# The opening of a gated cross-attention and MoE kernel: ctx laid out transposed, Wk in four quarters on SyncE's queue, x's first pair normed alone

## The reference

```python
q = (layernorm(x) @ Wq);  k = (context @ Wk * SCALE);  v = (context @ Wv)
attn = softmax(q k^T)                                   # 16 heads, 64 context tokens
x = x + tanh(g_xattn[0]) * ((attn v) @ Wo + bo)
h = layernorm(x);  probs = softmax(mean_t(h) @ gate_w);  top 2 experts, weights normed
x = x + tanh(g_ffn[0]) * sum_e combine[e] * (gelu(h @ w1[e] + b1[e]) @ w2[e] + b2[e])
```

## Time and profile before

| | |
|---|---|
| median of 3 runs | 322.09 us |
| the profiled execution, its time | 321.86 us |
| its span | 319.8 us |
| TensorE busy | 314.9 us, 98% |
| VectorE busy | 233.9 us, 73% |
| ScalarE busy | 164.1 us, 51% |
| GpSimd busy | 78.7 us, 25% |
| TensorE's granted clock | 1.0 of full speed throughout |

### The profile page before, as it was taken

One profiled execution on the slowest core, in us unless ns is written; L12 is line 12 of the kernel. 1 busy time (PEld: TensorE's weight loads), 2 busy tenths in 40 slices (PEclk: granted clock), 3 DMA queues, 4 the chain that ended last, 5 costly groups with the idle time before them and its releaser, 6 DMA issues.

```text
span 319.8 us, 5745 instructions
## 1 busy us (share of the span) xinstructions
PE 314.9 (98%) x1881; PEld 272.6 (85%) x1881; DVE 233.9 (73%) x563; ACT 164.1 (51%) x577; POOL 78.7 (25%) x158
## 2 busy tenths in 40 slices
PE   8999999999999999999999999999999999999996
PEld 8978988989999999888788888888887899888896
DVE  1989997988889999999998475466767554442643
ACT  2658556686765768766366254444543442321320
POOL 1416548484465535425600000000000000000000
PEclk9999999999999999999999999999999999999999
DMA  7991000000000027500016250000020000000011
GB/s 275 382 162 6 1 2 0 2 1 3 0 0 3 0 83 251 196 1 0 2 8 255 78 186 1 0 0 0 22 101 11 2 0 2 0 0 0 2 65 66
DMA packets 20765, 17.35 MB, mean 54 GB/s; under 512 B 11068, under 2 KB 16900, under 8 KB 20612
## 3 DMA queue, kind: packets, MB, share of 16 engines
q1 hardware_dynamic: 20464, 16.51, 17.2%
q10 hardware_dynamic: 276, 0.52, 0.5%
HBM read 14.93 MB, written 2.10 MB: 53 GB/s over the span
## 4 chain that ended last, share of the span: by engine, by line
PE 88%; DVE 7%; DMA 2%; issue 1%; ACT 1%; SPq 0%; DVEq 0%
PE ps L1105 26%; PE ps L1106 26%; PE ps L1107 26%; PE ps L1190 4%; DMA xt<-in_x_dram 2%; PE ps L1279 1%; PE ps L1125 1%; DVE mx L857 1%; PE ps L1163 1%; DVE pT_lo L815 1%; PE ps L1221 1%; PE ps L1377 1%; ACT sx L587 1%; DVE stats L736 1%; DVE sm L826 1%
## 5 line engine op out<-in xcount | busy, mean ns | idle before, releaser
L674 ACT ACTIVATE gel<-ps,b1sel 128x512 f32<-128x512 f32 x64 | 43.9, 690 | 95.5 <-PE ps L1107 95.4
L1064 DVE CAST h_hi<-gel 128x512 fp32r<-128x512 f32 x64 | 28.4, 444 | 58.7 <-ACT gel L674 58.4
L587 ACT ACTIVATE sx<-ps,mx 128x64 f32<-128x64 f32 x128 | 38.3, 327 | 27.6 <-DVE mx L857 27.6
L1105 PE MATMUL ps<-yT_hi,w_hi 128*128 128x512 f32 (+1 forms) x128 | 50.5, 395 | 0.0
L1106 PE MATMUL ps<-yT_lo,w_hi 128*128 128x512 f32 (+1 forms) x128 | 50.0, 391 | 0.0
L1107 PE MATMUL ps<-yT_hi,w_lo 128*128 128x512 f32 (+1 forms) x128 | 49.9, 390 | 0.0
L1066 DVE TENSOR_TENSOR h_lo<-gel,h_hi 128x512 fp32r<-128x512 f32 x64 | 44.9, 702 | 2.2
L473 POOL TENSOR_TENSOR sx<-sx,rs 128x512 f32<-128x512 f32 x32 | 33.1, 1056 | 48.1 <-DVE rs L831 48.0
L1105 PE MATMUL ps<-h_hi,w_hi 128*128 128x512 f32 x96 | 38.4, 400 | 0.0
L1107 PE MATMUL ps<-h_hi,w_lo 128*128 128x512 f32 x96 | 37.5, 390 | 0.0
L1106 PE MATMUL ps<-h_lo,w_hi 128*128 128x512 f32 x96 | 37.4, 390 | 0.0
(11 more groups left out here) (145 smaller groups left out, 673.7 us busy)
## 6 DMA issues: line engine op xcount, KB each, us to landing
stage_w<-in_L_ffn_w_dram SPq DMA_DIRECT2D x7, 1024.0 KB, 7.4
out_dram<-xt SPq DMA_DIRECT2D x6, 256.0 KB, 2.5
wqT<-in_L_xattn_Wq_dram SPq DMA_DIRECT2D x2, 512.0 KB, 6.8
wv_sb<-in_L_xattn_Wv_dram SPq DMA_DIRECT2D x2, 512.0 KB, 8.4
wo_sb<-in_L_xattn_Wo_dram SPq DMA_DIRECT2D x1, 1024.0 KB, 13.6
xt<-in_x_dram SPq DMA_DIRECT2D x1, 1024.0 KB, 11.0
stage_w<-in_L_ffn_w_dram SPq DMA_DIRECT2D x2, 512.0 KB, 4.4
wk_sb<-in_L_xattn_Wk_dram ACTq DMA_DIRECT2D x1, 512.0 KB, 4.4
```

The costliest lines, as they stand in the source:

```text
L587: last = nc.scalar.activation(sx[:, par, c0:c0 + M], ps[:, 2 * par + 1, c0 - BANK:c0 - BANK + M], ACT.Exp, bias=mx[:, par, h:h + 1], accum ...
L674: nc.scalar.activation(gel[:, f % 4, :], ps[:, h_bank, :], ACT.Gelu, bias=b1sel[:, b, slot, f:f + 1]).then_inc(gelu_done, 1)
L1064: nc.vector.tensor_copy(h_hi[:, f % 4, :], gel[:, f % 4, :]).then_inc(hhi_ready, 1)
L1105: mm(acc, hi_w, hi_x, start=start, stop=False)
```

## The change

Eight things change, all ahead of step 2:

- ctx comes from the host transposed, [128 rows of the width, 2, batch, 64], straight into `ctxT`; the group ctxT (two transposes on TensorE, a copy on VectorE) is gone. TensorE's 6 + 3 warm-up matmuls become 8.
- Wk comes in four quarters of 256 KB, each with a semaphore; kT waits for a quarter ahead of every second block. All four are issued by SyncE.
- SyncE's order is now ctx, Wk quarters 0 and 1, x's tiles 0 and 1, quarters 2 and 3, first half of Wq, x's tiles 2 and 3, second half of Wq, Wv and on as before.
- x's parts are now tiles 0 and 1, 2 and 3, 4 to 7, 8 to 15 (before: 0 to 3, 4 to 7, 8 to 15). VectorE does the whole norm of the first pair, then the statistics and the first part of the norm of the second pair, then goes on to tg.
- GpSimd makes the Newton steps of the second pair in step -1, after xn of tile 1.
- The statistics of tiles 6 and 7 move from the end of VectorE's opening to step 0, between the copy of vT's second group and the output bias.
- The banks of the opening's groups are dealt anew: before, kT, A0 to A7, vT were in 1, 2, 3, 4, 5, 6, 0, 1, 3, 4, 2, 6; now in 5, 6, 0, 2, 3, 4, 5, 6, 1, 2, 3, 6.
- TensorE's first transpose of xn waits for the identity matrix itself.

```diff
-        GRP_BANK = dict(zip(groups, [0, 1, 2, 3, 4, 5, 6, 0, 1, 3, 4, 2, 6, 4, 5, 0, 6] + [0, 1] * len(LATE)))
+        GRP_BANK = dict(zip(groups, [5, 6, 0, 2, 3, 4, 5, 6, 1, 2, 3, 6, 4, 5, 0, 6] + [0, 1] * len(LATE)))
...
-        X_PARTS = [(0, TB // 2), (TB // 2, TB), (TB, NT)]
-
-        X_BY_DVE = X_PARTS[1][0]
+        X_PARTS = [(0, 2), (2, TB // 2), (TB // 2, TB), (TB, NT)]
+
+        X_BY_DVE = X_PARTS[2][0]
...
-            sp.dma_start(ctx_sb[:, :], ctx_tokens.rearrange("b m d -> (b m) d")).then_inc(ld_ctx, 16)
-            load_x(0, 0, 0, 2)
-            sp.dma_start(wk_sb[:, :, HD // 2:HD], Wk[1].rearrange("k p n -> p k n")).then_inc(ld_wk[1], 16)
-            load_x(1, 0, 2, TB // 2)
+            sp.dma_start(ctxT[:, :, :, :], ctx_tokens).then_inc(ld_ctx, 16)
+            for quarter in range(4):
+                sp.dma_start(wk_sb[:, quarter, :, :], Wk[quarter]).then_inc(ld_wk[quarter], 16)
+                if quarter == 1:
+                    load_x(0, 0, 0, 2)
             for half in range(2):
                 blocks = slice(half * NP // 2, (half + 1) * NP // 2)
                 sp.dma_start(wqT[:, blocks, :], Wq[half]).then_inc(ld_wq[half], 16)
+                if half == 0:
+                    load_x(1, 0, 2, TB // 2)
...
+                if s == -1:
+                    newton(*X_PARTS[1], rstd1, ve_x, 2)
                 if s == 1:
-                    newton(*X_PARTS[1], rstd1, ve_x, 2)
+                    newton(*X_PARTS[2], rstd1, ve_x, 3)
                     pool.sem_inc(x_rstd, 1)
                 if s == 4:
-                    newton(*X_PARTS[2], rstd1, ve_x, 3)
+                    newton(*X_PARTS[3], rstd1, ve_x, 4)
...
-            act.dma_start(wk_sb[:, :, 0:HD // 2], Wk[0].rearrange("k p n -> p k n")).then_inc(ld_wk[0], 16)
...
-            group("ctxT", 0)
             x_stats(0, range(0, 2))
+            x_norm(0)
             x_stats(1, range(2, TB // 2))
-            x_norm(0)
+            x_norm(1)
...
-            x_stats(2, range(TB // 2, TB))
+            x_stats(2, range(TB // 2, TB // 2 + 2))
...
                 if s == 4:
-                    x_norm(2)
+                    x_norm(3)
...
                 if s == 0:
                     group("vT", 1)
+                    x_stats(2, range(TB // 2 + 2, TB))
                     out_bias(0)
-                    x_norm(1)
+                    x_norm(2)
...
+                pe.wait_ge(ld_ctx, 16)
+                if kind == "vT":
+                    pe.wait_ge(ld_wv[i], 16)
+                for m in range(4):
+                    quarter, c0 = 2 * i + m // 2, (4 * i + m) * P
+                    if kind == "kT" and m % 2 == 0:
+                        pe.wait_ge(ld_wk[quarter], 16)
                     for k in range(KD):
-                        last = nc.tensor.transpose(bank[:, k * P:(k + 1) * P], ctx_sb[:, k * P:(k + 1) * P], ident[:, :])
...
+                        w = wk_sb[:, quarter, k, m % 2 * P:(m % 2 + 1) * P] if kind == "kT" else wv_sb[:, k, c0:c0 + P]
+                        last = mm(bank[:, m * P:(m + 1) * P], w, ctxT[:, k, :, :].rearrange("p b j -> p (b j)"),
+                                  start=(k == 0), stop=(k == KD - 1))
...
-            warm_up(6)
-            group("ctxT", 0)
-            warm_up(3)
+            warm_up(8)
             group("kT", 0)
             group("kT", 1)
```

More of the change, by code:

```diff
@@ L17, in gated_cross_attention_moe_kernel @@
     P = 128
-    B, M, D = ctx_tokens.shape
-    S = out.shape[0] // B
+    _, _, B, M = ctx_tokens.shape
+    S, D = out.shape[0] // B, out.shape[1]
     HD = 2 * Wv.shape[-1]
@@ L113, in gated_cross_attention_moe_kernel @@
     first = [cursor[0]]
-    wk_sb = place("wk_sb", [P, KD, HD], at=first)
+    wk_sb = place("wk_sb", [P, 4, KD, HD // 4], at=first)
     wv_sb = place("wv_sb", [P, KD, HD], at=first)
@@ L119, in gated_cross_attention_moe_kernel @@
     vT_sb = place("vT_sb", [P, NP, B, M], at=first)
-    ctx_sb = place("ctx_sb", [P, D], at=first)
-    ctxT = place("ctxT", [P, KD, P], at=first)
+    ctxT = place("ctxT", [P, KD, B, M], at=first)
     first2 = [cursor[0]]
@@ L175, in gated_cross_attention_moe_kernel @@
         ld_wq = [sem(f"ld_wq_{i}") for i in range(2)]
-        ld_wk = [sem(f"ld_wk_{i}") for i in range(2)]
+        ld_wk = [sem(f"ld_wk_{i}") for i in range(4)]
         ld_x = [sem(f"ld_x_{i}") for i in range(4)]
@@ L298, in gated_cross_attention_moe_kernel @@
         late_groups = [(kind, i + odd) for kind, i in LATE.values() for odd in range(2)]
-        setup_groups = [("ctxT", 0), ("kT", 0), ("kT", 1)]
-        groups = setup_groups + A0 + V0 + late_groups
+        groups = [("kT", 0), ("kT", 1)] + A0 + V0 + late_groups
         number = {g: n for n, g in enumerate(groups)}
-        GRP_BANK = dict(zip(groups, [0, 1, 2, 3, 4, 5, 6, 0, 1, 3, 4, 2, 6, 4, 5, 0, 6] + [0, 1] * len(LATE)))
+        GRP_BANK = dict(zip(groups, [5, 6, 0, 2, 3, 4, 5, 6, 1, 2, 3, 6, 4, 5, 0, 6] + [0, 1] * len(LATE)))
         assert all(s % 2 == 1 for s in LATE)
@@ L749, in group @@
                 bank = ps[:, GRP_BANK[(kind, i)], :]
-                if kind == "ctxT":
-                    dve.wait_ge(grp_done, n + 1)
-                    nc.vector.tensor_copy(ctxT[:, :, :], bank[:, 0:D].rearrange("p (k i) -> p k i", k=KD)).then_inc(grp_dve, 1)
                 if kind == "vT":
@@ L1112, in group @@
                     wait_group_read(pe, *GRP_BEFORE[(kind, i)])
-                if kind == "ctxT":
-                    pe.wait_ge(ident_ready, 1)
-                    pe.wait_ge(ld_ctx, 16)
-                    for k in range(KD):
-                        last = nc.tensor.transpose(bank[:, k * P:(k + 1) * P], ctx_sb[:, k * P:(k + 1) * P], ident[:, :])
[L1118 to L1126, removed]
+                pe.wait_ge(ld_ctx, 16)
[5 more added lines that the diff above has]
+                        pe.wait_ge(ld_wk[quarter], 16)
+                    for k in range(KD):
+                        w = wk_sb[:, quarter, k, m % 2 * P:(m % 2 + 1) * P] if kind == "kT" else wv_sb[:, k, c0:c0 + P]
+                        last = mm(bank[:, m * P:(m + 1) * P], w, ctxT[:, k, :, :].rearrange("p b j -> p (b j)"),
+                                  start=(k == 0), stop=(k == KD - 1))
                 last.then_inc(grp_done, 1)
@@ L1215, in step @@
                     if t == 0:
+                        pe.wait_ge(ident_ready, 1)
                         pe.wait_ge(tg_ready, 1)
@@ L1445, in _laid_out @@
         a = a.T.reshape(2, -1, 128, a.shape[0]).transpose(0, 2, 1, 3)
-    if name in ("L0_xattn_Wk", "L0_xattn_Wv"):
+    if name == "ctx_1024":
+        a = a.transpose(2, 0, 1).reshape(-1, 128, *a.shape[:2]).transpose(1, 0, 2, 3)
+    if name == "L0_xattn_Wk":
+        a = a.reshape(a.shape[0] // 128, 128, 4, -1).transpose(2, 1, 0, 3)
+    if name == "L0_xattn_Wv":
         a = a.reshape(a.shape[0] // 128, 128, 2, -1).transpose(2, 0, 1, 3)
```

## The result

The changed kernel takes 326.00 us (median of 4, 325.52 to 326.63) against 322.08 us (median of 4): ratio 1.0121, 95% interval 1.0109 to 1.0134. Slower was forecast, but by 0.4%, to 323.3 us, and 326.0 lies outside the range of 321.9 to 324.1. Two thirds of the loss, some 2.7 us (3.92 - 1.26), were not in the sum.

What follows compares the result with a forecast made beforehand. TensorE, busy 98% of the span, bounds the kernel, its end set by the opening's chain through VectorE. Terms -0.03 + 0.95 + 0.34 = +1.26 us gave 323.3 us against 322.09; range 321.9 to 324.1.

Steps and rivals of the forecast that it cites:

- two places of the opening: Start of a_lo (11.76) and of the output bias (22.38); a shift of either is handed on whole to the end.
- Part 1: ctx transposed, no ctxT group: TensorE's side of the opening up to 0.72 us sooner, which alone frees nothing.
- The second small set: VectorE's statistics and first part for x's second pair: their fixed costs eat the 1.9 us head start.
- GpSimd's Newton steps: Second pair's steps, 3.7 us, run from 12.4 to about 16.1 or up to 1 us later; hidden by 4 us.
- x's first pair in use (5.95): VectorE's opening: start on x at 5.95 with one queue, bounds 5.86 and 6.78.
- the meeting: VectorE's second first part runs beside GpSimd's xn operations, which hold up its small operations: +0.95 us.
- statistics moved: Two statistics, 0.69 us, now before the output bias, where VectorE waited 0.35 us: +0.34 us.
- -0.03 for the order: VectorE's opening: the new order from x's statistics through tg gives 11.73 against 11.76.
- TensorE's wait before the last A pair up from 0.3 to over 1 us: Sign expected in the changed kernel's opening; a wait under 0.3 us would make the forecast wrong in sign.
- One queue starts later: Rival: x's first pair usable at 6.78, all of part 3 (VectorE's opening) moves by 0.83, 324.1 us; chance 0.09.
- the middle between two cases: VectorE's stops beside GpSimd: seam won, two stops, about +0.65 us; seam lost, three stops, +1.2; taken +0.95.
- luck of the seams: Rival: GpSimd and VectorE don't get in each other's way, a_lo at 11.73, 322.4 us; chance 0.22.

Runs made afterwards that it cites:

- run 6: Changed kernel with Wk's quarters 0 and 1 on ScalarE's queue, GpSimd's xn after VectorE's second first part, statistics of tiles 6 and 7 back in the opening: 321.69 us.
- run 3: Changed kernel with Wk's quarters 0 and 1 issued by ScalarE and x's first pair second on SyncE's queue: 323.00 us, ratio 1.0039.
- run 1: Changed kernel with GpSimd starting xn of tile 0 only after VectorE's second first part: 322.57 us, ratio 1.0011.
- run 5: Changed kernel with Wk's quarters 0 and 1 on ScalarE's queue and GpSimd's xn only after VectorE's second first part: 321.88 us, ratio 0.9989.
- run 2: Changed kernel with nine matmuls on zeros in TensorE's wait before the last A pair: 323.96 us, ratio 1.0064.
- run 7: Kernel before the change with ten linked small VectorE operations added at the end of the first norm: 324.90 us, ratio 1.0092.
- run 4: Changed kernel with the statistics of tiles 6 and 7 back at the end of VectorE's opening: 324.49 us, from 322.92 to 325.61.
- run 11: Changed kernel's loads, layout, banks and warm-up, with norm and statistics as in the kernel before: 325.45 us, ratio 1.0105.
- run 9: Changed kernel with x's first pair second on the one queue, ahead of all four quarters of Wk: 322.54 us, ratio 1.0008.
- run 10: Changed kernel with x's first pair second on one queue, GpSimd kept out of VectorE's second first part, statistics of tiles 6 and 7 back in the opening: 322.05 us.
- run 8: Kernel before the change with ten small VectorE operations added after the first norm and nine matmuls on zeros in TensorE's wait: 324.84 us.
- run 12: Second look at run 8, the same delayed and filled kernel before the change: 323.92 us.

## Why the prediction was wrong

Several steps held. TensorE's time is settled by two places of the opening and handed on whole: +4.06 us at the bias (26.44 against 22.38), +4.0 at pT_lo, +4.1 in the span. Part 1 was worth nothing on the path (run 6, where all of it stays, shows it as at best the 0.1 us by which the last pair is sooner). But a head start of TensorE is added to its wait: in run 3 it comes to the A groups at 9.27 instead of 9.94, which is 0.67 of its wait of 1.38 us. In the changed kernel it had none (10.05), since Wk's third quarter, forecast for 6.55, held it until 7.79, which cost nothing else. The second small set eats the head start: 5.72 us from the statistics to tg in run 1, where the working gives 5.66. GpSimd's Newton steps (13.94 to 17.6) stayed hidden.

The sum, term by term, against the changed kernel's profile:

| term | forecast us | measured us | from |
|---|---|---|---|
| x's first pair in use (5.95) | 0 | +1.04 | 6.99 |
| the meeting | +0.95 | +1.23 | 6.95 - 5.72 |
| statistics moved | +0.34 | +0.2 | 9.43 - 9.23, run 5 against 6 |
| TensorE's clock | none | +1.58 | 3.37 - 1.79, vT's first group |
| sum, with -0.03 for the order | +1.26 | +4.0 | span +4.1 |

**The step that failed is the sum's silence on TensorE's wait.** The prediction foresaw "TensorE's wait before the last A pair up from 0.3 to over 1 us" among its signs, and gave that wait the price of its length alone. A wait that takes TensorE to 2.35 us has a second price: matmuls at half the clock for more than 3 us. Run 2 shows it in the changed kernel (late VectorE kept, idle TensorE filled, no fall in four executions), run 7 in the kernel before (two falls in four). Taking for each kernel the wait of its profiled execution, the fall stands at waits of 1.4 us (run 3; two of eight fell, their own waits not seen), 2.0 (run 4, four of eight), 2.3 (changed kernel, four of four) and 2.6 (runs 7 and 11, two of four and at least three of four); with a wait of 1.2 us or less it never occurred (runs 1, 5, 6, 9 and 10, 53 executions). It costs 1.4 to 1.8 us. What decides within one kernel whether it falls isn't settled, and neither is the split of run 8.

**The second is a size: x's landing.** The sum took 5.95 and gave the later issue next to nothing, since "the issue is seldom what ends last". The case "One queue starts later", by which the issue's delay passes whole, was among the rivals, at 0.09, with 6.78 as its bound (and 323.35 + 0.83 = 324.2 us, not the 324.1 written there). The profiles bear it out. With these loads on one queue x's first pair was in use at 6.99, 6.78 (run 1), 6.39 (run 2), 6.46 (run 4) and 6.09 (run 11), 6.54 in the mean; with the same layout on two queues at 5.24, 5.59 and 5.64 (runs 3, 5 and 6), 5.49 in the mean. That is 1.05 us, and the issue is 0.93 us later. From issue to use it is 3.97 to 4.87 us on one queue and 4.05 to 4.46 on two. The rate has a small share at most: by 6.0 us the five had moved 1229 KB in the mean and the three 1282, an estimated 0.15 us. The bytes ahead count too, as the forecast said: in run 9, issued at 1.19 and with 512 KB less ahead of it on the one queue, the pair was in use at 4.42. No run moves the issue alone, so the split between issue and place is argued from these profiles, not shown. The 5.86 that the forecast started from was an early one as well: with the loads of the kernel before, runs 7, 8 and 12 have 6.54, 6.32 and 6.30.

The Trainium skill, DMA: Bandwidth & Descriptors, section "Issuing engines are not separate DMA queues", says that a second issuing engine saves issue time alone. The 0.93 us agree with it. The rates do not: from 6 to 10 us one queue moved 340 to 386 GB/s and two moved 403 to 408, although SyncE alone had asked for 2176 KB by 4.5 us, when less than 875 KB had been moved. What a single queue lacks there was not tried.

**The meeting was mis-sized, not misread.** I took the middle between two cases; the dearer one, three stops, came, and a GpSimd operation ended each. The Trainium skill, SBUF — State Buffer, section "Who interferes with whom" (the later of the two fully blocks), gave +1.2; the trace agrees with 1.23. It is no accident of one profile: from the first statistics to tg it is 6.94 or 6.95 us in the four profiles with the meeting (changed, runs 2, 3 and 4) and 5.72 or 5.73 in the three of the same order without it (runs 1, 5 and 6). What I called luck of the seams did not come in any of the four. Run 9 shows what does decide: whether GpSimd is done before VectorE comes to its second set, 0.4 us in that run.

The two late terms are one chain: each tenth by which x or VectorE was late was paid once as lateness, and together they took TensorE's wait to where its clock falls. That is why single cures look too good: runs 1, 3 and 9 gain 3.4, 3.0 and 3.5 us, together far more than the 3.9 there were to lose.

## What to carry to other kernels

Price a wait of TensorE in two parts: its length, and what the matmuls behind it take at half the clock if it falls, as it did behind the waits of 2.0 to 2.6 us here; an engine that comes early to the wait makes it longer. Some matmuls on zeros in the wait took the fall away in run 2; in run 8 they gained no time, so they have to be measured. Before you hand a second engine its share earlier, look what its operations will then run beside: small VectorE operations that read two tensors from SBUF stopped here for each GpSimd operation that they met. And when a load moves, count both the bytes ahead of it and how much later it is issued, and read its landing off more than one profile: the same loads gave 6.09 to 6.99. The first input that a chain needs goes ahead of the weights (run 9: 3.5 us for one line, the meeting and the fall of the clock that went with it included).

## What the runs showed of the hardware

The granted clock of TensorE falls to half after a wait of about 2 us in some executions and not in others of the same kernel, so such a kernel gets a wide spread (322.9 to 325.6 in run 4) where runs 1, 9 and 10 keep within 1.2 us. The row of the granted clock doesn't tell all of TensorE's pace: it reads 1.00 in the first 4 us, where a record of 128 columns takes 0.24 us instead of 0.12. One DMA queue moved 281 to 358 GB/s between 3 and 6 us and 340 to 386 between 6 and 10, where two moved 373 to 402 and 403 to 408. Three times in a row a two-column VectorE operation of 0.16 us with two inputs in SBUF took 0.53 to 0.58 us and ended with the GpSimd operation beside it, which itself kept its 0.61 us.
